# A two-layer graph network block: the first block's result rows are built while the last gathers still run

## The reference

```python
loops = jnp.arange(n, dtype=edge_index.dtype)
ei = jnp.concatenate([edge_index, jnp.stack([loops, loops])], axis=1)
src, dst = (ei[0], ei[1])
xp = (x @ W_gat).reshape(n, H, C)
a_src = jnp.einsum('nhc,hc->nh', xp, att_src)
a_dst = jnp.einsum('nhc,hc->nh', xp, att_dst)
alpha = jax.nn.leaky_relu(a_src[src] + a_dst[dst], NEG_SLOPE)
m = jax.ops.segment_max(alpha, dst, num_segments=n)
ea = jnp.exp(alpha - m[dst])
denom = jax.ops.segment_sum(ea, dst, num_segments=n)
attn = ea / (denom[dst] + 1e-16)
msg = xp[src] * attn[..., None]
out = jax.ops.segment_sum(msg, dst, num_segments=n)
...
h = layer_norm(h + x, g1, be1)
ff = jax.nn.relu(h @ w1 + b1) @ w2 + b2
return layer_norm(ff + h, g2, be2)
```

## Time and profile before

| | us |
|---|---|
| median of 3 runs | 3253.76 |
| lowest and highest of them | 3248.36, 3260.42 |
| the profiled execution, its own time | 3263.96 |
| its span | 3262.2 |

### The profile page before, as it was taken

How to read it: one execution, slowest core, us unless ns; L and a number is a source line. 1 busy time by engine, 2 the same in 40 slices (tenths; PEclk the granted TensorE clock), 3 DMA queues, 4 the chain that set the end, 5 groups by cost and what they waited for, 6 DMA issues and landing times.

```text
span 3262.2 us, 33511 instructions
## 1 busy us (share of the span) xinstructions
PE 2247.2 (69%) x10666; PEld 1570.5 (48%) x10666; DVE 1858.0 (57%) x3253; ACT 839.7 (26%) x1614; POOL 2458.8 (75%) x2011
## 2 busy tenths in 40 slices
PE   2787777747777777777777645747767547888740
PEld 1555555525555655565565534534444334454420
DVE  4889889983433433334334322346767567898720
ACT  1333233213322223223222222322222222222210
POOL 7778777887878878787787488888783075878877
PEclk9989889977888778777777766767888667888775
DMA  2333233221111112212111111111110110111100
GB/s 59 85 72 78 68 76 79 53 57 28 38 37 33 39 39 41 40 32 43 37 36 30 24 13 31 25 18 28 21 24 9 45 16 16 40 28 28 35 10 10
DMA packets 116212, 123.93 MB, mean 38 GB/s; under 512 B 70726, under 2 KB 72747, under 8 KB 116070
## 3 DMA queue, kind: packets, MB, share of 16 engines
q0 software_dynamic: 64000, 30.57, 10.0%
q1 hardware_dynamic: 52070, 91.52, 8.8%
HBM read 59.51 MB, written 64.00 MB: 38 GB/s over the span
## 4 chain that ended last, share of the span: by engine, by line
PE 35%; DVE 23%; POOL 22%; issue 11%; ACT 6%; SPq 2%; DMA 1%; DVEq 0%; ACTq 0%; POOLq 0%
POOL ring L430 15%; PE C L546 7%; PE V L534 7%; POOL out_rows L478 6%; PE C L510 5%; PE T L495 3%; DVE region L1595 3%; PE V L795 3%; DVE var L1235 3%; PE C L540 2%; PE C L542 2%; ACT sq L923 2%; DVE region L1587 2%; DVE region L1338 2%; ACT hid L934 2%
## 5 line engine op out<-in xcount | busy, mean ns | idle before, releaser
L430 POOL DMA_INDIRECT ring<-in_x,index x800 | 979.3, 1224 | 244.4 <-issue 243.2
L478 POOL DMA_INDIRECT out_rows<-ring,index_out x400 | 496.7, 1242 | 278.3 <-DVE ring L1407 158.9
L1235 DVE TENSOR_REDUCE var<-sq 125x16 f32<-125x512 f32 x325 | 220.7, 681 | 791.9 <-ACT sq L923 791.4
L452 POOL DMA_INDIRECT x_table<-region,index_out x400 | 483.3, 1208 | 152.4 <-issue 121.0
L430 POOL DMA_INDIRECT ring<-x_table,index x400 | 496.5, 1241 | 124.5 <-issue 123.9
L534 PE MATMUL V<-xT,w_q 128*128 128x500 f32 x600 | 369.0, 766 | 74.2 <-ACT hid L934 41.0
L923 ACT ACTIVATE sq<-C 125x512 f32<-125x512 f32 x300 | 179.4, 598 | 903.5 <-PE C L546 527.0
L510 PE MATMUL C<-center,xT 128*125 128x128 f32 x1400 | 246.2, 335 | 104.9 <-DVE hrow L1257 70.0
L546 PEld LDWEIGHTS C<-w_c,hid 128*125 128x125 f32 x2400 | 313.5, 215 | 0.0
L546 PE MATMUL C<-w_c,hid 128*125 128x32 f32 x2400 | 312.2, 293 | 0.0
L495 PE MATMUL T<-ident,hrow 125*128 125x125 f32 x1000 | 190.1, 328 | 164.0 <-DVE hrow L1251 139.0
(11 more groups left out here) (250 smaller groups left out, 3143.8 us busy)
## 6 DMA issues: line engine op xcount, KB each, us to landing
ring<-in_x,index POOLq DMA_INDIRECT x800, 3.3
nodes<-in_x SPq DMA_DIRECT2D x25, 500.0 KB
x_table<-nodes SPq DMA_DIRECT2D x25, 500.0 KB
x_plain<-nodes SPq DMA_DIRECT2D x25, 500.0 KB
nodes<-x_plain SPq DMA_DIRECT2D x50, 250.0 KB
out_rows<-nodes SPq DMA_DIRECT2D x50, 250.0 KB
x_table<-region,index_out POOLq DMA_INDIRECT x400, 2.6
ring<-x_table,index POOLq DMA_INDIRECT x400, 2.7
```

Source lines behind the costliest of these rows:

```text
L430: pool.indirect_dma_start(out=ring[0:P, j, s * F:(s + 1) * F], out_offset=None, in_=table, in_offset=bass.IndirectOffsetOnAxis(ap=index[0: ...
L452: pool.indirect_dma_start(out=x1_table[:, :], out_offset=bass.IndirectOffsetOnAxis(ap=index_out[0:P, j, s:s + 1], axis=0), in_=rows_out[0: ...
L478: pool.indirect_dma_start(out=out[:, :], out_offset=bass.IndirectOffsetOnAxis(ap=index_out[0:P, j, s:s + 1], axis=0), in_=ring[0:P, j, s * ...
L1235: v.tensor_reduce(unit(var, k), slots(squares(k)), AX.X, ALU.add).then_inc(var_ready, 1)
```

## The change

- The waves of stage D and the x chunks are written anew as one function `d_wave(w)` for 26 waves, with the steps of units, x chunk and y chunk interleaved on each engine rather than one behind the other.
- The 15 node units start one a wave in waves 0 to 14 and end in wave 16. They use the buffers 7, 8, 9 and 6 in turn.
- The joins of the first softmax are spread over waves 10 to 13 (before: behind 10 to 12). The x chunks of blocks 0 and 1 sit in waves 14 to 23 (before 13 to 22), and the tail of x block 1 is in wave 23 with its carry in wave 24, no longer in stage E.
- The y chunks of block 0 are summed and normalized in waves 20 to 24 and finished in waves 21 to 25.
- Finished y rows are written in place into `diff` (region1), and the scatters read them there and take their indices from `scatter_to`. So the copy of 16 indices and the wait for a free ring buffer are gone.
- Stage E starts with `y_second` (y chunks of block 1 with the joins of the last three blocks), then `e_block(2, None)`: the x chunks of block 2 with no y work beside them, then (3,2), (4,3), and block 4 alone.
- SP loads the first three destination buffers in wave 11 and the other two in wave 16, and POOL's scatter loop is written out (400 instructions in a row).

```diff
+JOIN_AT = NJ * EARLY
+X_FROM = JOIN_AT + 4
+Y_FROM = X_FROM + NJ + 1
...
+def wave(w):
+
+    at = {stage: w - lag for stage, lag in (("n3", 2), ("n2", 1), ("n1", 0)) if 0 <= w - lag < UD}
+    if X_FROM <= w < X_FROM + EARLY * NJ: at["x"] = w - X_FROM
+    if Y_FROM <= w < Y_FROM + NJ: at["y2"] = w - Y_FROM
+    if Y_FROM < w <= Y_FROM + NJ: at["y3"] = w - Y_FROM - 1
+    if w in (X_FROM + NJ, X_FROM + 2 * NJ): at["carry"] = (w - X_FROM) // NJ - 1
+    if w == JOIN_AT + 1: at["join"] = 0
+    if w == JOIN_AT + 3: at["join"] = 1
...
-            with pool.Fori(0, NB) as b:
-                for j in range(NJ):
-                    pool.wait_ge(ring_filled, b * NJ + j + 1)
-                    pool.sem_inc(cleared, 1)
...
+            for c in range(NC):
+                pool.wait_ge(ring_filled, c + 1)
+                pool.sem_inc(cleared, 1)
+                for s in range(CE):
+                    e = c * CE + s
+                    pool.indirect_dma_start(
+                        out=out[:, :], out_offset=bass.IndirectOffsetOnAxis(ap=scatter_to[0:P, e:e + 1], axis=0),
+                        in_=diff[0:P, e * F:(e + 1) * F], in_offset=None,
...
+            def d_wave(w):
...
+                if "y2" in at: y_sum(0, at["y2"])
+                if not first:
+                    dve.wait_ge(c_done, st["d1"] + 1 + CREDIT)
+                    logits_src(w - 1)
...
+                if "y2" in at: y_norm(2, norm["2"])
+                if not last:
+                    relu_rows(0, spread(0))
+                    st["d1"] = cq.at
...
+                if x: x_products(at["x"], 2, pending, V); x_sum(at["x"], pending)
...
+                if "y3" in at:
+                    y_finish(0, at["y3"], norm["3"])
+                if x:
+                    x_products(at["x"], 3, pending, V); x_sum(at["x"], pending); x_sum(at["x"], pending)
+                    if at["x"] % NJ == NJ - 1:
+                        x_tail(at["x"] // NJ)
...
-                y_finish(0, 3, spread(3))
-                x_tail(1)
-                y_finish(0, 4, spread(3))
-                x_carry(1)
...
+            e_block(EARLY, None)
+            for y in range(EARLY, NB):
                 e_block(y + 1 if y + 1 < NB else None, y)
```

530 lines of the change are left out of this document (257 added, 273 removed).

## The result

| | before | changed |
|---|---|---|
| median, us | 3263.05 (20 runs beside the changed kernel) | 3242.6 (20 runs) |
| lowest and highest | 3241.42, 3276.47 | 3224.43, 3308.39 |
| span of the profiled execution | 3262.2 | 3244.6 |

The ratio is 0.9933 with a 95% interval of 0.9916 to 0.9951: a gain of 0.7%, where 2.6% was forecast. One of the 20 runs, the one of 3308.39 us, fell into a slower state of the chip and is not in the ratio. The forecast of 3169 us was wrong, and its range (3130 to 3208) does not hold the time. The 3253.76 from which the forecast started was the median of three runs; over 20 runs the kernel before takes 9.3 us more, so the forecast's ratio of 0.974 would stand for 3178 here. That is an eighth of the miss of 73.6 us and does not explain it.

What follows compares the result with a forecast made beforehand. The prediction took the end to be bound by DVE's path to POOL's last wait, then POOL's scatters. Its terms, -27 - 13 + 77 - 121.5 = -84.5 us, took the median from 3253.8 to 3169 us; range 3130 to 3208.

Steps and rivals of the forecast that it cites:

- Term 1: When DVE leaves stage D: softmax over at 2250, then 242 us of work and 46 of waits; -27 us (-58 to +18).
- Term 2: Start of stage E: `y_second` in place of `y_first`, without an x block's tail and first load's wait; -13 us (-5 to -20).
- Terms 3 and 4: Stage E: x block 2 alone on DVE's path, +77 us; POOL with five chunks fewer behind its last wait, -121.5 us.
- (a): Rival: stage D gains nothing, its waits stay and DVE leaves at 2565 to 2575; 3196 to 3206 us; chance 0.20.
- (b): Rival: waits nearly vanish in stage D (2510) and `y_second` loses 20 us; 3134 us; chance 0.18.
- (e): Rival: POOL reaches its floor, with no wait at y chunk 10; 3090 us; chance 0.02.
- (c): Rival: the first ten chunks' 160 scatters slow down beside DVE, 2.18 us each; 3196 us; chance 0.04.
- (d): Rival: all 400 scatters slow down and POOL bounds from the gathers' end; slower than before, 3354 us; chance 0.03.

## Why the prediction was wrong

**What bounds the kernel** was read rightly. POOL's last wait stands ahead of y chunk 10, DVE's path sets its end, and POOL does not wait again: 363.2 us for 15 chunks, 24.2 each. y chunk 10 came 49.3 us after the part with x block 2 (2828.19 to 2877.5; 49.6 taken).

**Term 1** failed, in both of its halves.

- *"the joins are spread thinner, the backlog there is smaller, so I take 38 us instead of 49: 2250, at worst 2261."* It was 2277.8. The sentence looks at the backlog alone. It does not ask what is queued behind each join on PE and ACT. Spread over four waves, the softmax meets the head of a wave four times, at 4.90, 14.12, 8.16 and 19.94 us of PE's time. The edits that only move these meetings bring its end to 389.3 us after the first gather, or 2254.6 counted from the changed kernel's first gather. So the size was possible, but not in the order that the change wrote down.
- *"I take 3 us in each of ten x waves, 5 at the first (PE stands at the softmax), 4 in each carry wave, 8 in the last two: 51 at most, 46 taken."* DVE was idle for 89.0 us. Its work was 232.2, 10 less than summed up. The upper bound (the old 7.6 us in ten waves and some 15 more, 91) held the number; I took half of it with the argument that 12.7 us of x work are due at the wait and could fill it. But DVE's program is in order too, and the wait for which the argument was made is PE's and ACT's: `y_square` at the head of ACT's wave is an instruction of the change itself, and its place was to be seen in the code. Taking it out of the head of the wave gave 8.0 us in waves 20 to 23, twice. The sign that the prediction names for its own failure is there: waves 21 to 23 take 32.6 to 39.6 us, where 27 was to count as wrong.
- The gathers were not held back, as said: 621 us for the 25 chunks, where 618 were taken and the kernel before has 618.

**Term 2** has the right sign and most of its size: 9.0 us less, 13 taken. The missing 4 are less than the 7 us that TensorE's clock makes here: with the same 315 matmuls and 94 us of DVE work `y_second` takes either 148.3 or 141.5 us (below). In the kernels with the shorter one the term is -15.4 to -15.9.

**Terms 3 and 4** were right: +80.2 for +77, and -123.1 for -121.5.

**The rivals.** (a) came nearest: *"the waits stay, because DVE stands in order at squares and PSUM of PE whatever the order"*. Its mechanism is the one the traces show, with two flaws. Its size was bounded by the old time of leaving (2565 to 2575) as if the waits could only stay, while the change also added some; 2599.7 lay outside all cases. And "whatever the order" is false: with other orders DVE leaves at 680.1 us after the first gather, which would be 2545 in the changed kernel, and the whole takes 0.976 of the kernel before. The forecast was a ratio of 0.974. That the two ratios are close is in part luck: the better order has 62.2 us of idle time and not 46, and its shorter `y_second` gives 7 us back. (b) and (e) did not occur.

(c) and (d) fell with the scatters' median of 1.190 us, and their mechanism is visible mainly around the two joins of `y_second`. Five scatters in a row from 2631.29 take 1.88 to 2.72 us, and four in a row from 2700.71 take 1.88 to 2.44, while DVE runs its 125x1920 operations with two inputs in SBUF. The second place begins here:

```profile
2699.92 2.16 DVE L1558 TENSOR_TENSOR region<-head,carry 125x1920 f32<-125x1920 f32 x1
```

```profile
2703.45 1.88 POOL L507 DMA_INDIRECT out_rows<-region,scatter_to  x1 [0.30 <-issue]
2705.64 1.89 POOL L507 DMA_INDIRECT out_rows<-region,scatter_to  x1 [0.30 <-issue]
```

The Trainium skill, GPSIMD Engine Reference, Specifications, names this contention. The trace agrees at these places, and shows that the slowing does not reach the scatters at large: of the 400 eleven take between 1.85 and 2.8 us, and the chunks behind the last wait still take 24.2 us each, beside DVE operations of 125x512 with the same two SBUF inputs.

**The chances.** I gave 0.95 to "faster by over 0.5%". The gain of 0.7% lies on that side, but barely: its interval is 0.49 to 0.84%, and the median of 3242.6 is even above the 3237 that I had named as the edge, since that edge was reckoned from the three-run median. The range failed because its upper end was the far end of (a), and (a) was not priced by what the new order can add. Its own upper bound of term 1 (+18 instead of -27) would have given 3214. That bound was counted from 2250, and not from the 2261 that the same sum calls the worst of its first half: with both, DVE leaves at 2594, and 2599.7 was measured.

## What to carry to other kernels

When steps are spread over a loop that is written out by hand for several engines, price each one at the place where it stands in *every* engine's order: what must be ready there, when it will be, and what is queued behind it. Here the same work in a different order within its waves let DVE leave stage D 54 us earlier (680.1 instead of 734.4), three times the 17.0 us that the change itself took off the tail. A step whose input is made late in the wave before belongs behind the work that is ready at the wave's start. A wait that does not shrink can still have been made cheap, by what was moved ahead of it.

When experiments are compared by a mark at the end of a stage, look at the waves in between. Where two kernels have the same instructions in the same order in a wave and the wave differs, it is not the order that costs or saves: here TensorE's clock in two waves was worth 7 us, as much as most of the edits. And when work is left out to price it, look for what binds in its place: here it was the gathers, and the difference came out 10 us too small.

## What the runs showed of the hardware

**Two times for the same `y_second`.** It takes 148.2 to 148.3 us in six of the kernels and 141.4 to 141.9 in six (142.9 in the last), with the same 315 matmuls and DVE busy for 94 us in both. PE is busy for 80.04 us in one and 70.49 in the other, at a mean granted clock of 0.63 and 0.66. The two part at one spot, 25 to 28 us into it. The hidden layer's four matmuls of the second y chunk take 3.70 us in the changed kernel, at the lower of the two levels (1.2 GHz):

```profile
2627.50 3.70 PE L563 MATMUL V<-xT,w_q 128*128 128x500 f32 x4 [0.86 <-ACT xT L951]
```

and 1.95 us in the kernel with the joins later, at the higher one (2.4 GHz):

```profile
2599.35 1.95 PE L563 MATMUL V<-xT,w_q 128*128 128x500 f32 x4 [0.88 <-ACT xT L953]
```

PE had done the same instructions in the same order before it since the start of `y_second`, and the starts of the first of them (7.6 and 7.8 us after DVE's first instruction) differ by 0.25 us. What decides for the one or the other was not tried. It is a difference of 7 us that no edit aimed at, and a reader of single times would have credited it to the square. The last two waves of stage D show the same (above): the same 136 matmuls in 38.0 us at 0.68 and in 31.1 us at 0.88.

**One long issue.** In the kernel before one gather of stage D takes 6.27 us instead of 1.2. In the changed one, and in those with the joins and with the x tail later, there is such a gather too, and also one such scatter. In the changed kernel:

```profile
2407.88 6.49 POOL L459 DMA_INDIRECT ring<-x_table,index  x1 [0.30 <-issue]
...
2559.41 6.26 POOL L507 DMA_INDIRECT out_rows<-region,scatter_to  x1 [0.31 <-issue]
```

It is cheap here: no engine waits for the chunk behind that gather, and after the scatter POOL still waits 94.99 us. In the kernel with the x tail later and without y block 0 a second long one is the very last gather (7.04 us), and PE's wait of 12.88 us shown above ends with it. Its cause stays open.
